# Pieces of work between the expert jobs of a mixture-of-experts kernel, and the row fetches, begun in later slots

## The chip, the cores and the metric

The kernel runs on one core of a Trainium2 chip. The metric is the device time of one execution in microseconds (us). An engine here is one of TensorE (matmuls; PE in the profile, PEld for its weight loads), VectorE (DVE), ScalarE (ACT), GpSimd (POOL), and SyncE (SP), which only issues DMAs. Each has its own queue of instructions, executed in the order in which they are written; they wait for each other by semaphores.

## The reference

Four layers on x of shape (4, 512, 128), float32, each with a residual addition and a layer norm before it:

```python
x = x + attn_a(_layernorm(x), W)          # 16 heads of 8, squared scores with gated decay
x = x + ffn(_layernorm(x), ...)           # mixture of experts
x = x + attn_b(_layernorm(x), ...)        # a gated recurrence along the sequence
x = x + ffn(_layernorm(x), ...)           # the same mixture of experts

def ffn(x, gate_w, expert_bias, w1, w2, w3):
    scores = softmax(xf @ gate_w.T)
    _, sel = top_k(scores + expert_bias, 2)        # 2 of 8 experts for each of 2048 tokens
    routed = xf[token_idx] * top_scores_sorted[:, None]
    # per expert: h = silu(xe @ w1) * (xe @ w3); out = h @ w2, hidden width 352
    return zeros_like(xf).at[token_idx].add(routed_out)

def attn_b(x, ...):
    # i, f, g = x @ Wi, x @ Wf, x @ Wg; a causal convolution of 4 taps on i and f
    # h = sigmoid(f) * h + silu(i) * (1 - sigmoid(f)) along the sequence
    return (h * rms(h) * g_norm_weight * silu(g)) @ Wo
```

## The kernel before

The first attention layer takes the first 265 us. From there on the kernel is a sequence of 92 expert **jobs**. A job is 128 rows (pairs of token and expert) that go through one expert. The mixture of experts is done by halves of the tokens (two batches of 512 each), and twice, so there are four halves, m = 0 to 3, of 23 jobs (`JOBS`): 0 and 1 are the first expert layer, 2 and 3 the second. Job J is slot s of half m, with J = 23 m + s. The first four jobs stand among the attention's work, the rest is written as a loop over J on each engine (`job_tensor`, `job_scalar`, `job_vector`, `jobs_pool`).

In the slot of job J, TensorE does the two up matmuls of J (L1263, L1266), then the transposes (L1229: the product of job J-1; L1233: the rows of job J+1), then the down matmul of job J-2 (L1279). ScalarE does the silu of J (L1333), evicts the transposes (`turned`, L1245) and the result of J-2 (`ysb`, L1340). VectorE multiplies (`hid`, L1394). POOL issues the indirect DMA that returns the rows of J to `token_out` (L1185), waiting for `ysb`, and then the gathers of rows of later jobs (L1177) from `scaled_rows` into one of 12 buffers. A gather for the first job of a half waits for that half's ids (`id_in`) and for its scaled rows. Before a half's first transpose TensorE also waits for the list of experts (`s_job`, made by stage `experts`).

**Pieces between jobs.** Each engine calls `between_tensor`, `between_scalar`, `between_vector` or `between_pool` at the end of a slot. In the halves m = 1 and 2 these prepare half m + 1, whose tokens are the two batches b = 2m-2 and 2m-1:

- `add x` adds the returned rows of half m-1 to the residual (L1204, L1205), once SyncE has loaded them back after the last return of half m-1 has landed (`back_sync`, L1198). Then `stats x` (L187 to L192), the root on POOL (`norm_root`, L198), `apply x` (L205), `turn x` (transposes L212, eviction L221).
- the recurrence layer: `project` (L1480, L1484), `sigmoids`, `recur`, `squares`, `finish` (L1534, L1538), `means`, `rms_pool` (L1549), `out` (L1557).
- `stats y`, root, `apply y`, `turn y`: the norm of the second expert layer.
- routing: `logits`, `softmax`, `exp`, `top`, `first`, `second`, `ranks`, `weigh`, `scale` (L1019, followed by the stores of the scaled rows), `slots`, `spread` (to L1095), `lanes` (two operations, L1101), `number` (16 matmuls, L999, in two parts of eight that each wait for one `lanes`), `ids` (six operations from L1106 to L1111), `experts` (L1114 to L1117).

`IN_LATER` says in which slot each piece stands; a pair is for the first and the second batch. Within one slot the order is that of the calls: in `between_vector` the first batch's `recur` stands before the second batch's `apply x`, and in `between_tensor` both `project` pieces stand before `turn x`. Half 0 has its own table, `IN_FIRST`. In half 3 only the additions of the first two batches remain (`ADDS_IN_LAST`); those of the last two stand after the last job. The slots in which POOL's pieces stand are written as numbers in `between_pool`; a POOL piece at slot s comes after the return of job s, which exists two slots later on the other engines. `fetch_behind(J)` gives the job after whose return the rows of J are gathered.

## Time and profile before

| | |
|---|---|
| median of 3 runs | 662.81 us (662.61 to 666.58) |
| profiled execution | 668.38 us, of which 666.6 us are its span |
| TensorE busy | 515.2 us (77%), mean granted clock 0.845 |
| VectorE, ScalarE, POOL busy | 341.1, 322.3, 305.8 us |
| DMA | 44.01 MB, mean 66 GB/s |

How to read it: times are those of one profiled execution, from its first instruction on. A row of the timeline says when an instruction (or some merged ones of one line) starts, how long it lasts, engine, line and operation, and in brackets how long the engine was idle before it and which instruction released it. "remote" means that the semaphore came without an instruction of the profile that explains it. A clock of 1.00 is 2.4 GHz, 0.50 is 1.2 GHz; ends of matmuls are modelled. The time between two silus is the length of a slot.

### The profile page before, as it was taken

The page shows a single profiled execution, that of the slowest core. Times are in us where ns is not written, and L with a number is a line of the kernel's source. Part 1 is how long each engine was busy: PE and PEld are TensorE (multiplying, and loading weights), DVE is VectorE, ACT ScalarE, POOL GpSimd, SP SyncE. Part 2 cuts the span into 40 slices and gives each one's busy share as a digit, 9 for nine tenths or more (in the row PEclk, how much of TensorE's full clock was granted, in tenths as well). Part 3 has the DMA queues.
Part 4 walks back from the last instruction along what each step waited for, and adds up shares of the span by engine and source line. Part 5 has one row for each costly group of instructions (what it writes and reads, how often), then busy time and mean ns, then how long its engine had stood idle before and what let it go on. Part 6 is the DMA issues. An engine that isn't in the chain of part 4 may idle for free. (4 is left out here: it accounts for less than half of the span.)

```text
span 666.6 us, 11448 instructions
## 1 busy us (share of the span) xinstructions
PE 515.2 (77%) x3845; PEld 357.1 (54%) x3861; DVE 341.1 (51%) x798; ACT 322.3 (48%) x620; POOL 305.8 (46%) x320
## 2 busy tenths in 40 slices
PE   2756888789787878888958797785979878587792
PEld 1433465466465545676746466663746666365561
DVE  4657967977969885425614424361532536122111
ACT  1553676576568758366423224462422346233441
POOL 3111464454444477264464326426422743646531
PEclk9865588678678769998997998997889899789987
DMA  5055244244279302013013001122200212322203
GB/s 133 11 126 84 64 82 75 64 82 75 65 153 242 85 22 62 26 44 100 25 44 90 25 13 36 29 80 71 65 21 8 40 29 80 94 61 59 44 22 110
DMA packets 36442, 44.01 MB, mean 66 GB/s; under 512 B 5900, under 2 KB 31012, under 8 KB 36388
## 3 DMA queue, kind: packets, MB, share of 16 engines
q1 hardware_dynamic: 30500, 31.22, 19.2%
q0 software_dynamic: 5888, 12.07, 7.7%
q8 instruction: 34, 0.56, 0.4%
q14 instruction: 20, 0.16, 0.1%
HBM read 26.43 MB, written 15.86 MB: 63 GB/s over the span
## 5 line engine op out<-in xcount | busy, mean ns | idle before, releaser
L1185 POOL DMA_INDIRECT token_out<-ysb,id_out x92 | 94.4, 1026 | 160.0 <-ACT ysb L1340 142.7
L1394 DVE TENSOR_TENSOR hid<-silu,ps 128x352 f32<-128x352 f32 x92 | 47.9, 521 | 199.9 <-PE ps L1266 91.2
L845 POOL TENSOR_TENSOR PP<-PP,E 128x512 f32<-128x512 f32 x64 | 83.8, 1309 | 102.5 <-ACT PP L799 102.3
L1263 PE MATMUL ps<-room,turned 128*128 x184 | 84.4, 543 | 51.1 <-ACT turned L1245 34.5
L762 DVE TENSOR_SCALAR A<-ps 128x1024 int32<-128x1024 int32 x80 | 96.8, 1217 | 24.1 <-PE ps L669 23.8
L799 ACT ACTIVATE PP<-A,feps 128x1024 f32<-128x1024 f32 x80 | 92.1, 1151 | 26.7 <-DVE A L762 26.6
L1177 POOL DMA_INDIRECT tiled<-scaled_rows,id_in x92 | 91.2, 991 | 25.2 <-issue 23.5
L1245 ACT ACTIVATE turned<-ps 128x512 f32<-128x512 f32 (+2 forms) x100 | 56.3, 563 | 87.0 <-PE ps L1233 48.0
L1279 PE MATMUL ps<-room,turned 128*128 x552 | 83.9, 292 | 3.6 <-issue 1.8
L1279 PEld LDWEIGHTS ps<-room,turned 128*128 128x128 f32 x552 | 75.4, 207 | 5.5 <-issue 5.5
L1266 PE MATMUL ps<-room,turned 128*128 x184 | 78.3, 511 | 0.0
L1333 ACT ACTIVATE silu<-ps 128x352 f32<-128x352 f32 x92 | 42.6, 463 | 73.8 <-PE ps L1263 64.0
L669 PE MATMUL ps<-QS,KS 96*128 96x128 bf16 (+2 forms) x448 | 62.0, 286 | 17.2 <-DVE A L762 11.4
L1263 PEld LDWEIGHTS ps<-room,turned 128*128 128x128 f32 x184 | 30.4, 207 | 64.7 <-issue 64.5
L669 PEld LDWEIGHTS ps<-QS,KS 96*128 96x128 bf16 x448 | 38.9, 115 | 32.7 <-issue 17.5
L1229 PEld LDWEIGHTS ps<-ident,hid 128*128 128x128 f32 x276 | 39.0, 153 | 28.7 <-issue 20.3
L1266 PEld LDWEIGHTS ps<-room,turned 128*128 128x128 f32 x184 | 38.4, 209 | 22.6 <-issue 5.6
L1229 PE MATMUL ps<-ident,hid 128*128 128x128 f32 x276 | 50.1, 295 | 0.0
L808 ACT ACTIVATE E<-ps 128x512 f32<-128x512 f32 x64 | 37.9, 593 | 12.2 <-remote 8.7
L690 PE MATMUL ps<-QS,KS 6*128 6x128 bf16 x256 | 30.3, 250 | 17.1 <-ACT E L808 16.8
L1340 ACT ACTIVATE ysb<-ps 128x128 f32<-128x128 f32 x92 | 25.5, 277 | 27.8 <-PE ps L1279 14.8
L706 PE MATMUL ps<-PP,vp 128*9 128x128 f32 x768 | 35.2, 354 | 0.0
(196 smaller groups left out, 669.9 us busy)
## 6 DMA issues: line engine op xcount, KB each, us to landing
QS<-parts SPq DMA_DIRECT2D x24, 192.0 KB
KS<-parts SPq DMA_DIRECT2D x24, 192.0 KB
parts<-room SPq DMA_DIRECT2D x32, 128.0 KB, 2.4
scaled_rows<-xT SPq DMA_DIRECT2D x8, 512.0 KB
yb<-token_out SPq DMA_DIRECT2D x8, 512.0 KB, 4.1
room<-in_L_ffn_w_dram SPq DMA_DIRECT2D x2, 1408.0 KB, 14.3
tiled<-scaled_rows,id_in POOLq DMA_INDIRECT x92
token_out<-ysb,id_out POOLq DMA_INDIRECT x92
```

What stands on the lines that cost most here:

```text
L669: return pe.matmul(bank[:, col:col + width], KS[0:96, slot, h, P * j:P * j + P], QS[0:96, slot, h, t0:t0 + width], start=True, stop=True)
L762: v.tensor_scalar(A[:, U % 3, :].bitcast(I32), ps[:, bank:bank + 2, :].rearrange("p k t -> p (k t)").bitcast(I32), 0x7fffffff, None, ALU.b ...
L799: a.activation(PP[:, G % 2, 2 * p:2 * p + 2, :].rearrange("p k t -> p (k t)"), A[:, U % 3, :], ACT.Square, bias=feps[:, G // NG:G // NG + ...
L845: g.tensor_tensor(w, w, E[:, hh % 4, :], MUL).then_inc(s_PD, 1)
L1177: g.indirect_dma_start(rows[:, J % ROWS, :], None, xs_d[m], bass.IndirectOffsetOnAxis(ap=id_in[:, m % 2, s:s + 1], axis=0)).then_inc(s_row ...
L1185: g.indirect_dma_start(yr_d[m], bass.IndirectOffsetOnAxis(ap=id_out[:, m % 2, s:s + 1], axis=0), ysb[:, J % OUTS, :], None).then_inc(s_ret ...
L1229: ins = pe.transpose(ps[:, BK_R, P * c:P * c + P], hid[:, J % 2, P * c:P * c + P], ident[:, :])
L1245: a.activation(turned[:, n % 2, c0:c1, :].rearrange("p c l -> p (c l)"), ps[:, BK_R, P * c0:P * c1], ACT.Copy).then_inc(s_t, 1)
L1263: pe.matmul(ps[:, BK_A, 0:HID], turned[:, n % 2, 3, :], w13[:, bass.ds(e, 1), 0, :].squeeze(1), start=True, stop=True).then_inc(s_AB, 1)
L1266: pe.matmul(ps[:, BK_B + J % 2, 0:HID], turned[:, n % 2, 3, :], w13[:, bass.ds(e, 1), 1, :].squeeze(1), start=True, stop=True).then_inc(s_ ...
L1279: ins = pe.matmul(ps[:, BK_Y, 0:P], turned[0:hw, n % 2, c, :], w2s[0:hw, bass.ds(e, 1), c, :].squeeze(1), start=(c == 0), stop=(c == len(H ...
L1394: v.tensor_tensor(hid[:, J % 2, 0:HID], silu[:, J % 2, :], ps[:, BK_B + J % 2, 0:HID], MUL).then_inc(s_hid, 1)
```

## The change

The slots of all pieces in the halves 1 and 2, of the additions in half 3 and of POOL's pieces are renumbered, and the rule for the gathers. Nothing else is changed; the order in which pieces are called within a slot is the same.

```diff
-        IN_LATER = {'add x': (2, 4), 'stats x': (3, 5), 'apply x': (4, 6), 'turn x': (5, 6), 'project': (6, 7),
-                    'sigmoids': (6, 7), 'recur': (6, 7), 'squares': (7, 8), 'finish': (7, 8), 'means': (7, 9), 'out': (8, 10),
-                    'stats y': (9, 11), 'apply y': (10, 12), 'turn y': (11, 12),
-                    'logits': 13, 'softmax': 14, 'exp': 14, 'top': 15, 'first': 15, 'second': 16, 'ranks': 16, 'weigh': 17,
-                    'scale': (17, 18), 'slots': 17, 'spread': 18, 'lanes': (19, 20), 'number': 20, 'ids': 21, 'experts': 21}
-        ADDS_IN_LAST = (4, 6)
+        IN_LATER = {'add x': (5, 6), 'stats x': (6, 7), 'apply x': (7, 8), 'turn x': (8, 9), 'project': (9, 10),
+                    'sigmoids': (9, 10), 'recur': (9, 10), 'squares': (10, 11), 'finish': (10, 11), 'means': (10, 12), 'out': (11, 13),
+                    'stats y': (12, 14), 'apply y': (13, 15), 'turn y': (14, 15),
+                    'logits': 16, 'softmax': 17, 'exp': 17, 'top': 18, 'first': 18, 'second': 19, 'ranks': 19, 'weigh': 20,
+                    'scale': (20, 21), 'slots': 20, 'spread': 21, 'lanes': (21, 22), 'number': 22, 'ids': 22, 'experts': 22}
+        ADDS_IN_LAST = (6, 7)
...
                 b = 2 * m - 2
-                if s == 1:
+                if s == 4:
                     norm_root(2, b)
-                if s == 3:
+                if s == 5:
                     norm_root(2, b + 1)
-                if s == 5:
+                if s == 8:
                     rms_pool(b)
-                if s == 7:
+                if s == 10:
                     rms_pool(b + 1)
                     norm_root(3, b)
-                if s == 9:
+                if s == 12:
                     norm_root(3, b + 1)
...
             m, s = divmod(J, JOBS)
-            return J - ROWS if m == 0 else max(JOBS * m - 4 + s // 2, J - 9)
+            return J - ROWS if m == 0 else max(JOBS * m - 3 + s // 2, J - 9)
```

So not every piece moves by three: `add x`, `stats x` and `apply x` of the second batch move by two, `lanes` and `number` by two, `ids` and `experts` by one. The first gathers of a half (m > 0) stand behind the return of slot 20 of the half before instead of slot 19, two gathers behind each return; the double gathers now go on to the returns of slots 0, 1 and 2 of the half itself.

## Rows read from the trace of the kernel before

**Rows 1.** Timeline, silus of slots 2 to 4 of half 1: start, length, instruction, [idle before]

```profile
354.30 0.47 ACT L1333 ACTIVATE silu<-ps 128x352 f32<-128x352 f32 x1 [1.71 <-PE ps L1263]
...
358.06 0.46 ACT L1333 ACTIVATE silu<-ps 128x352 f32<-128x352 f32 x1 [0.32 <-PE ps L1263]
...
360.72 0.47 ACT L1333 ACTIVATE silu<-ps 128x352 f32<-128x352 f32 x1 [0.68 <-issue]
```

**Rows 2.** Waits: engine, line waited for, us in total, times, longest us

```profile
DVE yb L1204 <- DMA yb<-token_out: 10.4, 1, 10.4
```

**Rows 3.** Chain that ended last, its end: start, us, what

```profile
654.71 2.25 DMA token_out<-ysb,id_out
...
657.15 3.96 DMA yb<-token_out
```

**Rows 4.** Timeline, the seam from half 1 to half 2

```profile
448.47 0.17 DVE L1106 COPY idh<-ps 128x23 f32<-128x23 f32 x1
...
449.54 0.18 DVE L1111 TENSOR_SCALAR id_in<-idf 128x23 uint32<-128x23 f32 x1
...
450.04 0.47 ACT L1333 ACTIVATE silu<-ps 128x352 f32<-128x352 f32 x1 [0.68 <-PE ps L1263]
...
454.46 0.27 PE L1233 MATMUL ps<-ident,tiled 128*128 128x128 f32 x1
...
456.80 0.46 ACT L1333 ACTIVATE silu<-ps 128x352 f32<-128x352 f32 x1 [1.69 <-PE ps L1266]
```

**Rows 5.** Timeline, behind the first two seams

```profile
349.65 0.96 POOL L1177 DMA_INDIRECT tiled<-scaled_rows,id_in  x1 [0.30 <-issue]
...
351.99 0.60 ACT L1245 ACTIVATE turned<-ps 128x512 f32<-128x512 f32 x1 [5.95 <-remote]
...
463.69 0.95 POOL L1177 DMA_INDIRECT tiled<-scaled_rows,id_in  x1 [0.30 <-issue]
...
466.79 0.60 ACT L1245 ACTIVATE turned<-ps 128x512 f32<-128x512 f32 x1 [6.61 <-remote]
```

**Rows 6.** Windows: stretch, length, busy of PE, PEld, DVE, ACT, POOL, clock, DMA

```profile
457.00:473.50 16.50, 8.72 (x25) 5.97 (x26) 2.85 (x5) 2.96 (x8) 6.35 (x7) 0.59 0.28 93
```

**Rows 7.** Timeline, slot 6 of half 1

```profile
378.58 1.11 DVE L205 TENSOR_SCALAR xh<-xt,mv,lnr 128x128 f32<-128x128 f32 x4
...
379.83 0.63 PE L212 MATMUL ps<-ident,xh 128*128 128x128 f32 x4 [3.79 <-DVE xh L205]
```

**Rows 8.** Timeline, slots 18 to 20 of half 1

```profile
438.12 0.44 ACT L1333 ACTIVATE silu<-ps 128x352 f32<-128x352 f32 x1
...
441.24 0.54 DVE L1095 TENSOR_TENSOR injobid<-injob,idlo 128x368 bf16<-128x368 bf16 x1
...
441.94 0.45 ACT L1333 ACTIVATE silu<-ps 128x352 f32<-128x352 f32 x1
...
444.99 1.22 DVE L1101 TENSOR_TENSOR rest<-iolane,lane 128x1024 bf16<-128x1024 f32 x1
...
446.27 0.37 PE L999 MATMUL ps<-injobid,rest 128*128 128x46 bf16 x8 [0.50 <-DVE rest L1101]
```

**Rows 9.** The page's groups: out<-in xcount, busy us, mean ns, idle before, releaser

```profile
L1177 POOL DMA_INDIRECT tiled<-scaled_rows,id_in x92 | 91.2, 991 | 25.2 <-issue 23.5
...
L1394 DVE TENSOR_TENSOR hid<-silu,ps 128x352 f32<-128x352 f32 x92 | 47.9, 521 | 199.9 <-PE ps L1266 91.2
```

**Rows 10.** Timeline, the seam from half 0 to half 1

```profile
337.55 0.28 ACT L1340 ACTIVATE ysb<-ps 128x128 f32<-128x128 f32 x1 [0.18 <-PE ps L1279]
...
339.41 0.99 POOL L1185 DMA_INDIRECT token_out<-ysb,id_out  x1 [0.30 <-issue]
...
340.33 0.28 PE L1233 MATMUL ps<-ident,tiled 128*128 128x128 f32 x1
```

**Rows 11.** Timeline, slot 4 of half 1

```profile
362.87 1.04 POOL L198 TENSOR_TENSOR lnr<-lnv,mhalf 128x4 f32<-128x4 f32 x1
...
364.02 1.13 DVE L205 TENSOR_SCALAR xh<-xt,mv,lnr 128x128 f32<-128x128 f32 x4 [2.13 <-POOL lnr L198]
```

## Prediction

> **What bounds the kernel now.** The change acts only on the 88 jobs from about 265 us on, so I read the waits first, then this stretch in the timeline. TensorE sets its pace. A plain slot lasts 2.66 us from one silu to the next [rows 1]: TensorE runs the two up matmuls, the transposes and the down matmuls with hardly a gap, while ScalarE and VectorE wait for it. A piece between jobs costs time where TensorE works on it or is made to wait for it.
>
> The wait that a later start of the pieces would most plainly remove is the row addition's: VectorE needs the returned rows of the half before, and `mix_vector` stands behind it. The profile names such a wait once, 10.4 us [rows 2], and the end of the chain of waits tells which it is: a last return of 2.25 us, a load of 3.96 us and then the additions after the last job [rows 3]. Those additions are not touched. In the halves themselves the rows were there when VectorE came for them. So this gain is nothing in this execution, and the sum has to come from the rest.
>
> Three things do cost time around the pieces. First, the seam: between the last silu of half 1 and the first of half 2 lie 6.76 us instead of 2.66 [rows 4]. Second, just behind each seam, ScalarE's eviction of the transposes in slot 1 waited 5.95 us and 6.61 us [rows 5], and behind the third a little less, three waits of some 18 us together; the releaser is "remote", so the profile doesn't say what TensorE was held by. In the stretch after the second seam TensorE was busy 8.72 of 16.5 us, at a mean granted clock of 0.59 [rows 6]. Third, in slot 6 TensorE waits 3.79 us for the normalised rows of the second batch [rows 7].
>
> **The change, part by part.** No arithmetic is added. I follow one half of the two middle ones, m = 1, with its own times.
>
> *Slot 6, now 9.* Old: `recur` of the first batch and `apply x` of the second are both in slot 6, in this order, so VectorE normalises at 378.58 only after the recurrence, and TensorE's `turn x` has waited 3.79 us when it starts at 379.83 [rows 7]. New: `apply x` of the second batch is in slot 8, `turn x` in 9 behind the projection of the first, whose long matmuls hide it. The wait goes: -3.8 us in each middle half. Its lower bound is nothing, if VectorE gets late by as much (below).
>
> *The front.* Slots 0 to 4 carry nothing; three slots more of 2.66 us stand here, 8.0 us. At the back slots 18 to 22 become 21 and 22. Old, silu of slot 18 to silu of slot 22 is 438.12 to 450.04, 11.9 us; new, slot 21 does what slot 18 did, so 22 follows at the distance of the old 19, 438.12 to 441.94, 3.8 us [rows 4, 8]. 3.8 + 8.0 - 11.9 = -0.1 us.
>
> *The seam behind a middle half.* The ids of the next half were ready before its first gather; now they are on the path. Counted from the old slot 18 as the new slot 21: `spread` ends at 441.8 [rows 8]; `lanes` twice, 1.22 each, and the last job's product, 0.52, to 444.8 [rows 8, 9]; the second eight matmuls of `number`, 0.4, with the handover to 445.3 [rows 8]; the six operations of `ids`, which last from 448.47 to 449.72, 1.25 us [rows 4], and a handover, to 446.7. Then POOL may gather: issue to landing I take from the return, 2.25 us [rows 3], so the first row lies there at about 449.1. Old, the first row's transpose at 454.46 led to the silu at 456.80, 2.34 us later [rows 4]; so the first silu comes at 451.5, 9.5 us after the one at 441.94. Old 6.76: +2.8 us. TensorE also stands still in slot 22 for some 3 us, waiting for `lanes`; that lies inside these 9.5. `experts`, four operations behind `ids`, ends before the row lands and costs nothing; were the row earlier, it would be next. Bounds: +1.3 (the issue order alone, next part) to +4.
>
> *The seam before half 1.* There the ids are ready (its table isn't changed), and only `fetch_behind` acts: the first gather stands behind the return of slot 20, not 19. That result is in SBUF at 337.83, the return can start at 338.1 instead of 339.41 since no gathers stand before it [rows 10]; an indirect DMA occupies POOL 0.99 us, and 0.3 pass before the next [rows 9]; so gather at 339.4, landing at 341.7, against a transpose at 340.33 [rows 10]: +1.4 us. Bounds 0 and +2.6 (two places in POOL's queue).
>
> *POOL's queue at the front.* After a half's first three returns there are now two gathers each, then one. A return with two gathers is 3.85 us of POOL, with one 2.57, against slots of 2.66. From the first return on, the fourth (of slot 4, before the root of the first batch) starts 3 x 3.85 + 2.57 = 14.1 us later, the root ends at 16.4. The slots would have it wanted at about 11.0. Old, the root at 362.87 kept VectorE's normalisation waiting 2.13 us [rows 11], and TensorE hardly noticed. New, VectorE is blocked some 4.2 us in slot 7, with `stats` of the other batch and the next job's product queued behind; the normalised rows come at 17.6 where TensorE asks for them at 15.6. I take +1.8 us for each middle half; bounds 0 (the long first slots let POOL catch up) and +3.5.
>
> *Adds in the last half.* Two additions of 1.4 us move from slots 4 and 6 to 6 and 7; VectorE works only 0.52 us on each job there [rows 9], so nothing. What it costs without this cover is under 1 us. The outputs' stores start later, still long before the end of the last half.
>
> Sum: 1.4 + 2 x (2.8 - 0.1 + 1.8 - 3.8) = +2.8 us. The profiled execution took 668.38 us, 666.6 of it the span, 5.6 more than the median of 662.81; I set the sum against the median as it stands: 665.6.
>
> **The waits in slot 1.** The sum leaves the three unnamed waits as they were, and they are the largest thing nearby, some 18 us in all. Two readings fit. They ended shortly after POOL's last gather of its seam burst (349.65 + 0.96 against 351.99, and 463.69 + 0.95 against 466.79: 1.4 and 2.15 us [rows 5]), and the second of them ended 10.0 us after its half's first silu (456.80 to 466.79 [rows 4, 5]). If they hang on the burst of gathers and returns, they shorten. In the first seam it is nine instructions of 1.29 us from 338.1 on, to 349.4 instead of 350.6, while TensorE is 1.4 later: -2.6. In the others it is eight instructions from 446.9 to 456.9, 5.4 us after the first silu instead of 464.64 - 456.80 = 7.8: -2.4 each. Together -7.4 us. If they hang on TensorE's own time after its idle stretch, nothing changes.
>
> **The rivals.**
> - *The unnamed waits follow POOL's burst*: 2.8 - 7.4 = -4.6, 658 us. For it: both end shortly behind it [rows 5]. Against: the distance varies, 1.4 and 2.15. If they vanish altogether, 2.8 - 18 gives 648.
> - *The additions do wait in ordinary runs*, which are 5.6 us faster than the profiled one: perhaps these 5.6 us are just what gives the load its time. Then the change saves at most some 1.5 us a half more, 661. Against it: no row shows such a wait.
> - *The clock, on the other side.* TensorE now idles longer before the half's first job. The granted clock behind the second seam was 0.59 in the mean [rows 6], nearer to 1.2 than to 2.4 GHz, and the slot behind the first, partly at the lower level, took 354.30 to 358.06, 3.76 us, where a plain one takes 2.66 [rows 1]: +1.1, and +2 for a slot wholly at it. Two more such slots behind each of three seams are +12, with the sum 678 us; over 1% it gets from two more in all at +2. Against it: the clock is already low there, so much of this is paid.
>   The Trainium skill, "TensorE: Matmul & The Clock Gate", on the HAM clock gate, has it that "the default state is throttled, and activity releases the throttle": by that rule the longer idle would lead to this rival, while five plain slots in front would help the clock back. The trace agrees as far as low clocks stand behind the seams.
> - *It does not do what it says*: the additions never waited, so the parts merely trade places. This is the case that I forecast, with small bills.
>
> **How the numbers follow.** Unnamed waits stay, sum as above: 0.47. They shorten with the burst: 0.18; vanish or nearly: 0.1. Additions wait in ordinary runs: 0.1. Clock: 0.15. The likeliest gives 665.6; with its own bounds, 1.4 or 0 to 2.6 for the first seam and from both ends of the others, it runs from 655 to 671. I put 665. The range 655 to 672 leaves out the vanishing waits below and most of the clock case above. One per cent is 6.6 us, about what a measurement of this kernel tells from no change. Faster by more: the vanishing waits and a part of the burst case, 0.18. Slower by more: the clock case and the tail of the sum, 0.18. Within: 0.64.
>
> **What would show it.** TensorE's wait for the normalised rows of the second batch in slot 9 is gone; VectorE's wait for POOL's root in slot 7 is about 4 us instead of 2.13; TensorE stands before `number` in slot 22; seams of about 9.5 us behind the middle halves, 1.4 more at the first; no wait of the row additions in either kernel. I would be wrong if the evictions in slot 1 waited much less or more than 5 to 6.6 us, or if the clock behind the seams fell further.

## The result and the profile after

| | before | after |
|---|---|---|
| median | 664.69 us (4 runs, 662.61 to 669.22) | 641.53 us (4 runs, 639.94 to 646.65) |
| profiled execution | 668.38 us, span 666.6 | 639.94 us, span 638.2 |
| TensorE busy, mean granted clock | 515.2 us, 0.845 | 494.3 us, 0.879 |

The ratio is 0.9656, with an interval of 0.9577 to 0.9735: faster, by 3.4%. Ratios and their intervals are taken without the slower executions of each kernel, so a ratio can differ from that of the medians beside it, and the profile of the kernel before is of a slower one, 5.6 us above the median on record ahead of the prediction.

I had said 665 us, in a range of 655 to 672. The range missed the time, and the forecast of no change was wrong on this chip. On two of the three other chips on which both kernels ran, their ratio was 1.0144 and 1.0037, on the third 0.9817; the experiments below show where the difference lies.

I measure both kernels by the starts of their 92 silus (L1333). "Seam" is from the silu of slot 22 to that of slot 0 of the next half, "slots 1 to 3" from the silu of slot 0 to that of slot 3, "slots 4 to 22" from that of slot 3 to that of slot 22. In us:

| | first silu | half 0 | seam | slots 1-3 | 4-22 | seam | slots 1-3 | 4-22 | seam | slots 1-3 | 4-22 | last silu |
|---|---|---|---|---|---|---|---|---|---|---|---|---|
| before | 265.8 | 70.1 | 6.0 | 16.1 | 92.0 | 6.8 | 16.7 | 92.6 | 7.1 | 16.3 | 60.1 | 649.6 |
| after | 259.1 | 69.7 | 8.1 | 8.7 | 89.2 | 9.8 | 8.0 | 88.3 | 9.8 | 9.3 | 60.9 | 621.0 |
| change | -6.7 | -0.4 | +2.0 | -7.4 | -2.7 | +3.0 | -8.7 | -4.4 | +2.7 | -7.0 | +0.9 | -28.6 |

From the first silu to the last it is -21.8 us: slots 1 to 3 give -23.0, the seams cost +7.8, the rest gives -6.6. The 6.7 us ahead of the first silu lie in the attention, which the change doesn't touch.

The first seam, against [rows 10]: timeline of the kernel after; start, length, instruction, idle before it and its releaser.

```profile
328.85 0.46 ACT L1333 ACTIVATE silu<-ps 128x352 f32<-128x352 f32 x1 [0.68 <-PE ps L1263]
...
332.26 0.99 POOL L1177 DMA_INDIRECT tiled<-scaled_rows,id_in  x1 [0.30 <-issue]
...
335.07 0.30 PE L1233 MATMUL ps<-ident,tiled 128*128 128x128 f32 x1 [1.69 <-DMA tiled<-scaled_rows,id_in]
...
336.93 0.46 ACT L1333 ACTIVATE silu<-ps 128x352 f32<-128x352 f32 x1 [1.24 <-PE ps L1263]
```

TensorE now waits 1.69 us for the first row, whose gather stands one return later. Just behind it, against [rows 1, 5] (same view):

```profile
340.26 0.47 ACT L1333 ACTIVATE silu<-ps 128x352 f32<-128x352 f32 x1 [1.71 <-issue]
...
342.98 0.46 ACT L1333 ACTIVATE silu<-ps 128x352 f32<-128x352 f32 x1 [1.03 <-issue]
...
344.00 0.60 ACT L1245 ACTIVATE turned<-ps 128x512 f32<-128x512 f32 x1 [0.56 <-PE ps L1233]
...
345.63 0.46 ACT L1333 ACTIVATE silu<-ps 128x352 f32<-128x352 f32 x1 [0.68 <-PE ps L1263]
...
356.75 0.60 ACT L1245 ACTIVATE turned<-ps 128x512 f32<-128x512 f32 x1 [3.70 <-remote]
```

The wait of 5.95 us in slot 1 is gone; the eviction comes 0.56 us after ScalarE's last work. But the kind of wait is not gone: a "remote" one of 3.70 us stands 13 us later. The unnamed waits in the list of waits, which before has as 32.8, 18.1 and 6.0 us for the same three lines (us in total, times, longest us):

```profile
ACT turned L1245 <- remote: 19.3, 7, 3.7
...
DVE hid L1394 <- remote: 14.9, 3, 5.9
...
ACT ysb L1340 <- remote: 10.6, 7, 2.5
```

The seam behind half 1, against [rows 4, 8]:

```profile
434.88 0.44 ACT L1333 ACTIVATE silu<-ps 128x352 f32<-128x352 f32 x1
...
437.48 0.37 PE L999 MATMUL ps<-injobid,rest 128*128 128x46 bf16 x8 [1.11 <-DVE rest L1101]
...
438.96 0.18 DVE L1111 TENSOR_SCALAR id_in<-idf 128x23 uint32<-128x23 f32 x1
...
439.42 0.99 POOL L1177 DMA_INDIRECT tiled<-scaled_rows,id_in  x1 [2.33 <-DVE id_in L1111]
...
442.20 0.45 PE L1233 MATMUL ps<-ident,tiled 128*128 128x128 f32 x1 [1.11 <-DMA tiled<-scaled_rows,id_in]
...
444.67 0.46 ACT L1333 ACTIVATE silu<-ps 128x352 f32<-128x352 f32 x1 [1.71 <-PE ps L1263]
```

This is the chain as worked out: `lanes`, `number`, `ids`, gather, first transpose. It takes 9.79 us from silu to silu, where I had 9.5. The stretch behind it, against [rows 6] (windows; busy us of PE, PEld, DVE, ACT, POOL, then the clock):

```profile
442.00:458.50 16.50, 14.09 (x60) 9.28 (x61) 2.60 (x5) 5.81 (x13) 10.62 (x11) 0.88 0.36 109
```

TensorE is busy 14.09 us of the 16.5 instead of 8.72, at a granted clock of 0.88 instead of 0.59.

The pieces of half 1, against [rows 7, 11], and the end, against [rows 2, 3] (timeline, then the chain that ended last, then the waits):

```profile
363.69 1.04 POOL L198 TENSOR_TENSOR lnr<-lnv,mhalf 128x4 f32<-128x4 f32 x1
364.84 1.14 DVE L205 TENSOR_SCALAR xh<-xt,mv,lnr 128x128 f32<-128x128 f32 x4 [0.88 <-POOL lnr L198]
...
377.20 0.60 PE L212 MATMUL ps<-ident,xh 128*128 128x128 f32 x4
```

```profile
626.15 2.24 DMA token_out<-ysb,id_out
628.58 4.11 DMA yb<-token_out
```

```profile
DVE yb L1204 <- DMA yb<-token_out: 10.5, 1, 10.5
```

TensorE takes up `turn x` of the second batch without a wait, where it had waited 3.79 us. The end is unchanged, and GpSimd's gathers cost what they did [rows 9]:

```profile
L1177 POOL DMA_INDIRECT tiled<-scaled_rows,id_in x92 | 91.0, 989 | 29.3 <-issue 23.3
```

### The profile page after: what moved, and what is told of

The parts are those of the page before. It is cut to its first block and busy times, and to the rows that moved or that the text cites. A ratio compares the mean times of both kernels' runs of the same rounds, so it can differ in the third digit from the quotient of the medians.

```text
span 638.2 us, 11448 instructions
## 1 busy us (share of the span) xinstructions
PE 494.3 (77%) x3845; PEld 343.4 (54%) x3861; DVE 340.3 (53%) x798; ACT 321.6 (50%) x620; POOL 303.0 (47%) x320
## 5 line engine op out<-in xcount | busy, mean ns | idle before, releaser
L1185 POOL DMA_INDIRECT token_out<-ysb,id_out x92 | 92.0, 1000 | 136.7 <-ACT ysb L1340 121.8
L1263 PE MATMUL ps<-room,turned 128*128 x184 | 83.3, 536 | 39.6 <-ACT turned L1245 20.5
L1279 PE MATMUL ps<-room,turned 128*128 x552 | 80.3, 283 | 5.1 <-ACT ysb L1340 4.8
L1333 ACT ACTIVATE silu<-ps 128x352 f32<-128x352 f32 x92 | 42.5, 462 | 67.3 <-PE ps L1263 54.0
L669 PE MATMUL ps<-QS,KS 96*128 96x128 bf16 (+2 forms) x448 | 61.1, 283 | 18.5 <-DVE A L762 11.8
L1279 PEld LDWEIGHTS ps<-room,turned 128*128 128x128 f32 x552 | 71.4, 197 | 7.0 <-issue 7.0
L1266 PE MATMUL ps<-room,turned 128*128 x184 | 74.6, 489 | 0.0
L1263 PEld LDWEIGHTS ps<-room,turned 128*128 128x128 f32 x184 | 29.4, 201 | 54.8 <-issue 54.6
L1229 PEld LDWEIGHTS ps<-ident,hid 128*128 128x128 f32 x276 | 36.5, 144 | 25.2 <-issue 15.6
L1266 PEld LDWEIGHTS ps<-room,turned 128*128 128x128 f32 x184 | 37.7, 205 | 22.1 <-issue 4.5
L1229 PE MATMUL ps<-ident,hid 128*128 128x128 f32 x276 | 46.6, 279 | 0.1
L808 ACT ACTIVATE E<-ps 128x512 f32<-128x512 f32 x64 | 37.9, 592 | 13.9 <-remote 9.8
L1340 ACT ACTIVATE ysb<-ps 128x128 f32<-128x128 f32 x92 | 25.5, 277 | 27.9 <-remote 10.6
L690 PEld LDWEIGHTS ps<-QS,KS 6*128 6x128 bf16 x256 | 16.9, 105 | 32.5 <-ACT E L808 26.2
## 6 DMA issues: line engine op xcount, KB each, us to landing
room<-in_L_ffn_w_dram SPq DMA_DIRECT2D x2, 1408.0 KB, 13.9
```

The lines of the kernel that those rows point to most:

```text
L669: return pe.matmul(bank[:, col:col + width], KS[0:96, slot, h, P * j:P * j + P], QS[0:96, slot, h, t0:t0 + width], start=True, stop=True)
L1185: g.indirect_dma_start(yr_d[m], bass.IndirectOffsetOnAxis(ap=id_out[:, m % 2, s:s + 1], axis=0), ysb[:, J % OUTS, :], None).then_inc(s_ret ...
L1229: ins = pe.transpose(ps[:, BK_R, P * c:P * c + P], hid[:, J % 2, P * c:P * c + P], ident[:, :])
L1263: pe.matmul(ps[:, BK_A, 0:HID], turned[:, n % 2, 3, :], w13[:, bass.ds(e, 1), 0, :].squeeze(1), start=True, stop=True).then_inc(s_AB, 1)
L1266: pe.matmul(ps[:, BK_B + J % 2, 0:HID], turned[:, n % 2, 3, :], w13[:, bass.ds(e, 1), 1, :].squeeze(1), start=True, stop=True).then_inc(s_ ...
L1279: ins = pe.matmul(ps[:, BK_Y, 0:P], turned[0:hw, n % 2, c, :], w2s[0:hw, bass.ds(e, 1), c, :].squeeze(1), start=(c == 0), stop=(c == len(H ...
```

## The experiments

The question was what makes the unnamed waits. An eviction that waits for "remote" starts up to several us after the end that the profile models for TensorE's matmuls; I call such a result **late**, by the time from that end to the start of the instruction that waits for it. In the kernel before, the late ones in slot 1 stand at the end of GpSimd's unbroken runs of 12 gathers and returns, 15 us each (first seam: 335.6 to 350.6, result at 351.99). The kernel after has a run of nine, 11 us, then a pause of 3 us, then another of nine; its late results stand in the second, from some 7 us into it on (`ysb` at 352.42, `turned` at 356.75). Theory A: the length of GpSimd's run makes TensorE's results late. Theory B: the slots of the pieces matter. Theory C: the clock.

These runs were made on five chips, 2 to 6 here in order; chip 1 is that of the result, which may be one of them. A ratio is always to before on the same chip. Only on chips 1, 4 and 5 is there a profile of before, so on chips 2, 3 and 6 the slots can be set only beside profiles from other chips.

**The two halves of the change** (chip 2; before there 657.66 us).

```diff
fetch_only:
-            return J - ROWS if m == 0 else max(JOBS * m - 4 + s // 2, J - 9)
+            return J - ROWS if m == 0 else max(JOBS * m - 3 + s // 2, J - 9)
pieces_only: the whole change, but with the old line for the fetches
```

> The kernel before with the new rule for the gathers alone (first gather of a half behind the return of slot 20 instead of 19). The pieces stay in their old slots. Theory A, the unnamed waits behind the seams come from POOL's run of back-to-back gathers and returns (12 instructions, 15 us in the kernel before, 8 or 9 in the kernel after): they go with this edit, 18 to 23 us less, about 643 us. Theory B, the pieces' slots did it: 1 to 4 us more than before from the later first rows, 664 to 668 us. Theory C, the granted clock behind the seams: TensorE's idle time is about as long as before, so no change, 660 to 666 us.

> The changed kernel with the old rule for the gathers: all pieces and the additions in their new slots, first gather behind the return of slot 19. Theory A: the run at the seam from half 0 to 1 is as long as before and its wait of about 6 us stays there; behind halves 1 and 2 the first gather waits for the ids, returns 20 to 22 queue behind it, so the run is long again and the waits stay, 660 to 668 us. Theory B: the gain is here, about 643 us. Theory C: 660 to 668 us.

`fetch_only`: 643.07 us, ratio 0.9766 (0.9684 to 0.9848). In its profile, of an execution of 652.10 us, slots 1 to 3 take 8.3, 9.1 and 9.4 us, the seams 8.6, 8.7 and 8.7. `pieces_only`: 651.45 us, ratio 1.0014 (0.9961 to 1.0067). Its slots 1 to 3 take 15.2, 12.1 and 11.9, its slots 4 to 22 86.8 and 87.8. The eviction in slot 1 (`fetch_only`, then `pieces_only`; timeline):

```profile
351.07 0.60 ACT L1245 ACTIVATE turned<-ps 128x512 f32<-128x512 f32 x1 [0.56 <-PE ps L1233]
```

```profile
350.03 0.60 ACT L1245 ACTIVATE turned<-ps 128x512 f32<-128x512 f32 x1 [5.93 <-remote]
```

So on this chip the gain is the one line of the fetches, and B falls: the pieces alone give none. Beside the first profile of before they gain within the halves (92.0 and 92.6 there) and give it back at the seams (9.8 and 10.6 against 6.8 and 7.1); that before took 92 us on this chip too is not shown (chip 5 has 88.0 and 87.6).

**More work for TensorE behind the seam** (chip 2). Six idle fp32 matmuls of 128 columns stand ahead of the up matmuls of slots 0 to 2.

```diff
+        def fill_tensor():
+            for k in range(6):
+                nc.tensor.matmul(ps[:, BK_I, 0:P], ident[:, :], ident[:, :], start=True, stop=True)
...
+            if m and s < 3:
+                fill_tensor()
```

> The kernel before with six idle matmuls of 128 columns ahead of the up matmuls in the first three slots of halves 1 to 3, into a free PSUM bank; their results are used by nobody. Theory C, the clock falls in TensorE's idle time at the seams and that makes the long waits: the clock stays at 1.00 behind the seams and the waits shrink, 645 to 658 us. Theory A: the waits stay; the fillers cost up to 0.7 us a slot, 663 to 672 us.

665.66 us, ratio 1.0124 (1.0014 to 1.0233). The seams grow to 11.8, 11.8 and 13.9 us, slots 1 to 3 still take 11.7, 12.7 and 11.4, and results are still late; here the first silu (L1339 in this kernel):

```profile
343.55 0.47 ACT L1339 ACTIVATE silu<-ps 128x352 f32<-128x352 f32 x1 [6.34 <-remote]
```

C falls: the granted clock was 1.00 for at least 25 us ahead of each of the three late first silus. The stretch ahead of the one at 343.55 (windows; busy us of PE, PEld, DVE, ACT, POOL, then the clock):

```profile
315.00:343.50 28.50, 24.39 (x158) 18.80 (x157) 9.56 (x28) 10.62 (x26) 15.19 (x16) 1.00 0.11 35
```

The same holds from 434.0 to 459.6 and from 499.0 to 573.2 us. So the waits begin at the full clock, and it falls to the lower level only at or behind their ends.

**One gather behind each return** (chip 2), with the rows of J behind the return of J - 4.

```diff
-            return J - ROWS if m == 0 else max(JOBS * m - 4 + s // 2, J - 9)
+            return J - ROWS if m == 0 else J - 4
```

> The kernel before with the gathers of halves 1 to 3 one behind each return, the rows of job J behind the return of job J-4, so that POOL has two indirect DMAs for each slot of 2.66 us and no pairs of gathers at the seams. Theory A: the unnamed waits at the seams go or shrink below 2 us each, 640 to 650 us. Theories B and C: no gain from it; rows come at the last moment, 663 to 675 us.

814.32 us, ratio 1.2419 (1.2318 to 1.252). This was my mistake. TensorE transposes the rows of J + 1 in the slot of J, and these are gathered only after the result of J - 3 has gone out, so every slot waits for a gather:

```profile
PE ps L1233 <- DMA tiled<-scaled_rows,id_in: 128.2, 53, 4.8
```

Slots 1 to 3 took 9.2, 7.3 and 7.4 us. One late result is left behind the seams: at the first, `turned` at 342.03 is late by 1.9 us, at the end of a run of eight in 10 us. TensorE was so idle in this kernel that little more follows.

**Shorter runs** (chip 3; before there 645.86 us, 637.65 to 662.87).

```diff
after_lead6, from after:
-            return J - ROWS if m == 0 else max(JOBS * m - 3 + s // 2, J - 9)
+            return J - ROWS if m == 0 else max(JOBS * m - 3 + s // 2, J - 6)
six_first, from before:
-            return J - ROWS if m == 0 else max(JOBS * m - 4 + s // 2, J - 9)
+            return J - ROWS if m == 0 else max(JOBS * m - 4 + s // 2 + (s >= 6), J - 9)
```

> The kernel after, with the fetch rule max(23m - 3 + s//2, J - 6): behind the returns of slots 20, 21, 22 two gathers each, then one behind each return, so six are under way ahead of a half instead of nine in slots -3 to 2. Theory A (GpSimd's long unbroken runs of indirect DMAs make the results of TensorE come late): the second run behind each seam of the kernel after (345.2 to 356.6 us, nine instructions, late result 4.8 us at its end) breaks up, since every slot now has one return and one gather, 2.3 us of a 2.66 us slot; the late evictions behind it (4.8, 4.6, 3.4 us) shrink to 2 us or less, and the kernel gains 2 to 8 us on the kernel after: ratio 0.955 to 0.965 to the kernel before where the kernel after stands at 0.966 to 0.97. Rival (the late results have nothing to do with the length of the runs): the late evictions stay in the same slots and the time is that of the kernel after within 2 us. Either way the later start of slots 4 to 8's gathers costs nothing if rows land six slots (16 us) ahead of use against a landing of 2.3 us.

> The kernel before, with one number of the fetch rule changed: from slot 6 on a row is gathered one return later, so the first gathers of a half start as early as before (behind the return of slot 19 of the half before), and six instead of eight stand before the half's own first return; the pieces are where they were. Theory A (length of GpSimd's unbroken run): the run of twelve instructions, 15 us, at each seam becomes shorter or gets a pause, the late evictions in slot 1 (6.2, 5.3, 3.8 us) shrink or vanish, slots 1 to 3 behind each seam take 8 to 11 us instead of 16, and the ratio to before comes to 0.97 to 0.985. Rival (it matters that the first gathers of a half stand behind a later return, so that TensorE itself starts the half later): nothing changes, slots 1 to 3 stay at 16 us and the ratio at 1.00.

`after_lead6`: 634.58 us, ratio 0.9874 (0.974 to 1.0009). Slots 1 to 3 have no late result; the first ones stand in slots 5 to 7 and are down to 1.2 to 1.8 us. Further on there are some of 2.0 and 2.1 us in the middle halves and up to 2.6 in half 3. Slots 4 to 22 take 82.4 and 86.0 us. The ratio is short of the 0.955 to 0.965 that I expected. `six_first`: 654.3 us, ratio 1.0228 (1.0148 to 1.0308): a miss. Its run is ten instructions, 12.5 us; slots 1 to 3 take 14.2, 12.9 and 13.7 us, with results late by 4.8, 3.4 and 2.9 us. The late results are smaller than with the run of twelve on chip 1, as A has it, yet the kernel was 2.3% slower than before on this chip. Before itself was some 19 us faster here than on chip 1 (medians of 645.86 and 664.69), and that was the first sign that it is not the same on every chip.

**More GpSimd work in a quiet stretch** (chip 3). Behind each return of slots 14 to 21 of half 3, where gathers have ended, stands one idle gather, or one idle power.

```diff
idle_gathers, from after:
+                if m == 3 and 14 <= s < 22:
+                    nc.gpsimd.indirect_dma_start(junk[:, s - 14, :], None, xs_d[m],
+                                                 bass.IndirectOffsetOnAxis(ap=id_in[:, m % 2, s:s + 1], axis=0)).then_inc(s_junk, 16)
idle_powers, from after:
+                if m == 3 and 14 <= s < 22:
+                    nc.gpsimd.tensor_tensor(junk[:, s - 14, 0:TB], lnv[:, 0:TB], mhalf[:, 0:TB], ALU.pow)
```

> The kernel after, with one idle extra gather (its rows go to a buffer that nobody reads) behind each return of slots 14 to 21 of half 3, a stretch where a slot takes a plain 2.66 us and no piece stands between jobs. It takes GpSimd from about 2.3 us to 3.6 us for each slot; eight of them are 10.3 us more work for GpSimd, of which it makes up 0.35 us a slot. Theory A (dense indirect DMAs make TensorE's results late): evictions or products late by 2 us and more appear in this stretch, where the kernel after has none over 1 us, and TensorE's slots there lengthen before any buffer runs out. Rival B (only the buffers that GpSimd fills late can hold TensorE): rows are gathered nine slots ahead, so a delay of 10 us never reaches the first engine; slots stay at 2.66 us, and the end moves by the late last returns alone, 0 to 3 us.

> The kernel after, with one idle power operation of GpSimd (128 x 4... elements, about 1.0 us, result not read) behind each return of slots 14 to 21 of half 3 in place of the extra gather: GpSimd is as busy without a pause, but with no more DMAs. Theory A in the form that counts GpSimd's DMAs (their descriptors or packets): no late evictions, slots of 2.66 us, time of the kernel after. Theory A in the form that counts GpSimd's unbroken busy time: late results by 2 us and more, as in the run with idle gathers. If neither shows them, the long runs of this kernel's seams need something else as well, such as the loads and stores at the seam.

647.56 and 647.32 us (two runs each; after was not run on this chip, so the times say nothing). The first added instruction is behind the return at 615.8 and 618.3 us. `ysb` there, first with gathers (its line is L1342), then with powers (L1341):

```profile
619.22 0.28 ACT L1342 ACTIVATE ysb<-ps 128x128 f32<-128x128 f32 x1 [2.27 <-remote]
...
628.36 0.28 ACT L1342 ACTIVATE ysb<-ps 128x128 f32<-128x128 f32 x1 [2.25 <-remote]
```

```profile
620.37 0.28 ACT L1341 ACTIVATE ysb<-ps 128x128 f32<-128x128 f32 x1 [0.88 <-PE ps L1280]
...
630.19 0.28 ACT L1341 ACTIVATE ysb<-ps 128x128 f32<-128x128 f32 x1
```

With gathers there is a late result in every third slot or so. With powers, each about as long as a gather (1.05 us), only the first `ysb` is late, by some 0.4 us: the interval into slot 18 is 3.10 us, and those behind it are plain. The kernel after without any addition has the same there on chips 5 and 6 (3.07 and 3.09 us), where its gathers have ended. That speaks for the DMAs and against the mere busy time. It is one profile of each, so a pointer, not a proof. In both, three slots of the stretch ahead, where each return has its gather, took 9.0 to 9.1 us instead of 3 x 2.66.

**All on one chip again** (chip 4; before there 633.0 us, 622.08 to 637.2).

```diff
after_triple, from after:
-            return J - ROWS if m == 0 else max(JOBS * m - 3 + s // 2, J - 9)
+            return J - ROWS if m == 0 else max(JOBS * m - 3 + s // 3, J - 9)
before_again, after_again: unchanged; lead6_again: after_lead6
```

> The kernel before once more, for a second profile of it and its own spread beside the three others on this chip. Theory A (a long unbroken run of indirect DMAs on GpSimd makes results of TensorE late): the run of twelve at each seam, 15 us, is in the program, so the three late evictions of the transposes in slot 1 are there again, 3.8 to 6.2 us late each, and slots 1 to 3 behind each seam take 15 to 17 us, whatever the time of the execution. Rival (they were a matter of that one execution, as its time of 668 us beside runs of 638 to 666 would allow): they are absent or half as long, and then the gain of the change was luck of the executions compared. Time 640 to 665 us, ratio 1.00.

> The kernel after once more, on the same chip. Theory A: slots 1 to 3 behind the seams take 8 to 9.5 us again (before 16), the seams 8.1, 9.8 and 9.8 us, late results come at the end of the second run of nine behind each seam, 3.4 to 4.8 us; the ratio to before is 0.965 to 0.98. Rival (luck of the executions compared): the ratio is within 0.99 to 1.01.

> The kernel after with the fetch rule max(23m - 3 + s//3, J - 9): behind the returns of slots 20, 21 and 22 stand three gathers each instead of two, and none or one behind the next ones; so the gathers start at the same place, but all nine are in the first run: 12 instructions and some 15 us without a pause, as in the kernel before, where the kernel after has 8 or 9 and 10 to 11 us. Theory A: the late evictions in slot 1 come back, 3 to 6 us each, slots 1 to 3 take 12 to 16 us instead of 8 to 9, and the ratio to before is 0.985 to 1.0. Rival (the place of the first gather behind the return of slot 20 is what mattered, not the length of the run): slots 1 to 3 stay at 8 to 9.5 us, the time is that of the kernel after within 3 us, and the second run behind the seam is shorter.

> The kernel after with one gather behind each return from slot 0 on (rule max(23m - 3 + s//2, J - 6)), once more, on the same chip as the kernel after. Theory A: it has fewer late results than the kernel after and is 3 to 9 us faster, ratio to before 0.955 to 0.97. Rival (the 7 us between the two profiles was spread of the executions): within 2 us of the kernel after.

| chip 4 | median | seam | slots 1-3 | 4-22 | seam | slots 1-3 | 4-22 | seam | slots 1-3 | 4-22 |
|---|---|---|---|---|---|---|---|---|---|---|
| before_again | 634.93 | 6.5 | 8.7 | 94.3 | 6.0 | 7.3 | 99.3 | 6.0 | 7.3 | 50.4 |
| after_again | 633.26 | 8.7 | 9.4 | 90.2 | 9.8 | 9.3 | 90.3 | 10.3 | 9.0 | 50.5 |
| after_triple | 615.92 | 8.0 | 8.7 | 82.8 | 9.8 | 8.0 | 81.2 | 9.9 | 9.3 | 50.5 |
| lead6_again | 616.78 | 8.7 | 9.3 | 82.9 | 9.8 | 8.0 | 81.2 | 9.9 | 8.0 | 50.5 |

Theory A fell here, and my expectations for all four missed. **No result of TensorE is late, in any of the four**: the lists of waits have no "remote" row for `turned`, `hid` or `ysb`. The runs of indirect DMAs are even longer than on chip 1, since no late result interrupts them: in `before_again` 16 in 20.6 us at the first seam, and 43 in 55.1 us in half 3. The last half's 19 plain intervals take 50.4 us, 2.65 each, instead of 60. And before and after are equal: after has 1.0144 (1.0017 to 1.0271) to before, and before run again has 1.0155 (1.0035 to 1.0274) to itself, which is how far two sets of one kernel lie apart here.

Three more things are plain once the late results are out of the way. First, the additions do wait in the kernel before (`before_again`; SPq is the load's issue):

```profile
344.29 0.80 SPq L1198 DMA_DIRECT2D yb<-token_out  x2
344.37 0.60 ACT L1245 ACTIVATE turned<-ps 128x512 f32<-128x512 f32 x1 [0.56 <-PE ps L1233]
...
348.70 0.69 DVE L1204 TENSOR_TENSOR yb<-yb 128x512 f32<-128x512 f32 x1 [4.18 <-DMA yb<-token_out]
```

```profile
459.08 0.69 DVE L1204 TENSOR_TENSOR yb<-yb 128x512 f32<-128x512 f32 x1 [6.91 <-DMA yb<-token_out]
```

```profile
DVE yb L1204 <- DMA yb<-token_out: 21.8, 4, 10.4
```

Second, the root is late in the kernel after. The first batch's normalisation in `after_again`, then in `after_triple`:

```profile
361.93 1.13 DVE L205 TENSOR_SCALAR xh<-xt,mv,lnr 128x128 f32<-128x128 f32 x4 [4.17 <-POOL lnr L198]
...
363.21 0.63 PE L212 MATMUL ps<-ident,xh 128*128 128x128 f32 x4 [2.79 <-DVE xh L205]
```

```profile
357.63 1.13 DVE L205 TENSOR_SCALAR xh<-xt,mv,lnr 128x128 f32<-128x128 f32 x4 [0.87 <-POOL lnr L198]
...
359.25 0.60 PE L212 MATMUL ps<-ident,xh 128*128 128x128 f32 x4
```

Third, much of what separates the kernels on this chip is the clock that TensorE was granted. Slot 9 to slot 10 of half 1 in `after_again` and in `after_triple`, then the three slots with the recurrence (slots 6 to 9) in `before_again` and the same work (slots 9 to 12) in `after_triple` (windows):

```profile
364.47:376.56 12.09, 12.09 (x37) 6.77 (x36) 3.56 (x9) 3.56 (x8) 5.99 (x6) 0.86 0.11 33
```

```profile
360.49:370.92 10.43, 10.43 (x37) 5.63 (x36) 3.25 (x9) 3.56 (x7) 5.73 (x6) 1.00 0.14 40
```

```profile
355.72:390.16 34.44, 29.87 (x115) 18.20 (x114) 11.73 (x30) 9.23 (x19) 10.87 (x12) 0.90 0.06 18
```

```profile
360.49:388.06 27.57, 26.79 (x115) 16.25 (x114) 10.02 (x21) 9.07 (x18) 10.54 (x11) 1.00 0.09 22
```

The matmuls are the same in number, and TensorE is busy 1.7 and 3.1 us longer with them where the clock was lower.

**A fifth chip** (before there 651.22 us, 639.39 to 660.49).

> The kernel before, a third profile. What the runs have left open is whether the late results of TensorE (no instruction explains them; 16 us for slots 1 to 3 behind each seam, 60 us for the 19 intervals of the last half's slots 3 to 22) go with the chip or with the kernel. They were in the first profiles and absent (8.7, 7.3, 7.3 us and 50.4 us) in the one beside which before and after took 633 us alike. Theory D (they are a matter of the chip, or of what goes on beside on it, and of the density of GpSimd's DMAs only where they are there at all): in one call all kernels have them or none has; with them before takes 650 to 669 us, without 622 to 640. Theory A (length of the run alone): not tenable any more, since a run of twelve showed none.

> The kernel after, a third profile. Theory D: if before_third shows late results, this one shows them too, with slots 1 to 3 at 8 to 9.5 us against 16, and the ratio is 0.96 to 0.98; if before_third shows none, this one shows none either, the ratio is 0.99 to 1.02, and the parts come out as in the clean pair: seams 8.7, 9.8, 10.3 us against 6.5, 6.0, 6.0; the middle halves from slot 3 to slot 22 at 90.3 us each against 94.3 and 99.3. Rival (execution by execution, whatever the chip): one has them and the other not.

> The kernel after with three gathers each behind the returns of slots 20, 21 and 22 (rule max(23m - 3 + s//3, J - 9)), once more. Root theory (the returns of slots 0 to 2 with two gathers each push the root of the first batch back in GpSimd's queue, and VectorE's normalisation and TensorE behind it with it; 5.71 + 12.10 us for slots 9 and 10 of the kernel after against 2.73 + 10.44 here): without late results 14 to 20 us faster than the kernel after, ratio 0.97 to 0.98. Theory A, where late results are there at all: its run of twelve brings back those in slot 1, slots 1 to 3 take 12 to 16 us, and it loses some 15 us of that lead. Rival: the lead is there with late results too.

| chip 5 | median | seam | slots 1-3 | 4-22 | seam | slots 1-3 | 4-22 | seam | slots 1-3 | 4-22 |
|---|---|---|---|---|---|---|---|---|---|---|
| before_third | 642.83 | 6.8 | 11.8 | 88.0 | 6.0 | 12.9 | 87.6 | 7.1 | 13.0 | 55.4 |
| after_third | 646.06 | 8.7 | 9.0 | 93.4 | 9.8 | 9.3 | 90.0 | 9.8 | 7.9 | 58.3 |
| triple_again | 643.78 | 8.7 | 12.7 | 82.8 | 10.0 | 12.0 | 84.9 | 9.8 | 10.5 | 60.7 |

Late results are there in all three, where chip 4 had them in none of four, so they don't go with the single execution (theory D). Whether they go with the chip or with the time at which it ran, and what else ran on it then, is not shown: each chip was used at one time only. The waits of `before_third`, whose row for `yb` has 11.4 us, one of 10.4 being the last one:

```profile
ACT turned L1245 <- remote: 15.9, 5, 4.5
...
DVE yb L1204 <- DMA yb<-token_out: 11.4, 3, 10.4
```

They are milder than on the first chip, and the ratio of after is 1.0037 (0.9968 to 1.0105), not the 0.96 to 0.98 that I had expected with late results. `triple_again` has them in slot 2, at the end of its run of 12:

```profile
350.44 0.60 ACT L1245 ACTIVATE turned<-ps 128x512 f32<-128x512 f32 x1 [3.46 <-remote]
```

and its slots 1 to 3 take 12.7, 12.0 and 10.5 us where chip 4 had 8.7, 8.0 and 9.3. So where a chip has late results, the length of the run decides whether they stand in slots 1 to 3; where it has none, the length is nothing. It doesn't decide what they cost in all: `after_third`, with runs of nine, has its late results in slots 5 to 8 instead, and slots 4 to 22 take 93.4 us there where `triple_again` has 82.8. The lead of `triple_again` over after is 2 us here and was 17 us there.

**Two versions on a sixth chip** (before there 652.86 us). `one_earlier` is after with every piece of the halves 1 and 2 one slot earlier, and the fetch rule of `after_triple`.

```diff
one_earlier, from after:
-        IN_LATER = {'add x': (5, 6), 'stats x': (6, 7), 'apply x': (7, 8), 'turn x': (8, 9), 'project': (9, 10),
+        IN_LATER = {'add x': (4, 5), 'stats x': (5, 6), 'apply x': (6, 7), 'turn x': (7, 8), 'project': (8, 9),
...
-                    'scale': (20, 21), 'slots': 20, 'spread': 21, 'lanes': (21, 22), 'number': 22, 'ids': 22, 'experts': 22}
+                    'scale': (19, 20), 'slots': 19, 'spread': 20, 'lanes': (20, 21), 'number': 21, 'ids': 21, 'experts': 21}
...
-            return J - ROWS if m == 0 else max(JOBS * m - 3 + s // 2, J - 9)
+            return J - ROWS if m == 0 else max(JOBS * m - 3 + s // 3, J - 9)
```

> The kernel after with every piece of the halves 1 and 2 one slot earlier (ids and experts of the next half in slot 21, additions in 4 and 5, GpSimd's pieces one return earlier) and the rule max(23m - 3 + s//3, J - 9), so that the gathers stand behind the returns of slots 20, 21, 22, three each. What the parts should give against the kernel after: the ids are ready before the return of slot 20 has gone, so the two seams behind middle halves go from 9.8 us to 7 to 8 us (-2 to -3 each); the additions in slot 4 find the rows loaded, since SyncE's load starts in slot 1 and lasts 4 us; the root stands behind no double gathers, so slots 9 and 10 of the kernel after lose 4.6 us a half where that chip has no late results. Sum: 12 to 18 us faster than the kernel after without late results; with late results its run of twelve brings some 3 to 4 us in slots 3 and 4 of each half, and the lead is 3 to 8 us.

> The kernel after with one gather behind each return from slot 0 on (max(23m - 3 + s//2, J - 6)). Theory (the long run of GpSimd's DMAs matters only on chips with late results, the late root everywhere): 14 to 19 us faster than the kernel after on a chip without late results, as in the earlier call (616.8 against 633.3), 5 to 10 us on one with them. Rival: equal to the kernel after there.

> The kernel after on a fifth chip, to set the two beside it and for the ratio to before. Theory D: the ratio goes by whether TensorE's results come late on this chip: with strong ones (slots 1 to 3 of before 16 us) 0.965 to 0.975, without 1.00 to 1.01, in between 0.985 to 1.0. This kernel's own slots 1 to 3 take 8 to 9.4 us in any case, and the seams 8.1 to 8.7, 9.8 and 9.8 to 10.3 us.

After: 641.21 us, ratio 0.9817 (0.9727 to 0.9908), with late results in its profile. `lead6_third`: 629.42 us, ratio 0.9651 (0.9556 to 0.9746). `one_earlier`: 647.52 us, ratio 0.9916 (0.9867 to 0.9965), 6 us slower than after: a miss. Its seams fall only to 9.4 and 8.9 us (9.8 and 10.4), while its run of 12 puts slots 1 to 3 at 12.7, 13.5 and 11.8 us (8.7, 8.0, 9.1). Against after, `lead6_third` gains in slots 4 to 22, 83.2 and 84.4 us instead of 89.2 and 88.3. It was the faster one by 16.5 us on chip 4 and by 11.8 here, and below before on all three chips on which it ran, though on two of them the interval just takes in 1: the version to keep.

## Why the prediction was wrong

**The failed step: the unnamed waits were left as they were.** It carried 0.47 of the chances, against 0.28 for the two cases in which they change. On the first chip they vanished from slots 1 to 3, -23.0 us in a net of -21.8. The rival "vanish" gave 648 us, with 0.1; the rival "follow the burst" had the right mechanism for this chip but priced it at -7.4 us in all, because it let a wait end a fixed time behind the burst. In fact, cut from twelve to eight or nine with a pause behind it, the run made no late result at all in this profile. What I read wrongly was [rows 5]. I had three waits of the same kind at the same place and took "the profile doesn't say" for "it stays". A stretch of 18 us whose cause isn't known, beside a change that moves the gathers in it, should have had a wide range on the fast side. Even the stated bounds of the sum, 655 to 671, don't follow from its parts: these give -5.2 to +17.4 us, or 657.6 to 680.2, and the measured 641.53 lies below either. What makes the waits, and so why they went, stays open; that the line of the fetches is what removes them, the two halves of the change show on chip 2.

**"The additions wait in ordinary runs", 0.1, was true where results come in time.** On chip 4 VectorE waits 4.18 and 6.91 us in the kernel before. The interval into slot 5 is 4.33 us in half 1, and those into slots 5 and 6 are 8.34 and 3.88 us in half 2, against 2.66: 8.6 us together. In the profile that I had, TensorE's late results gave the load its time [rows 2]. The row was rightly read for this execution; it did not hold for the program.

**The seams were right.** First seam: +1.4 predicted, +2.0 measured, +2.2 on chip 4. Behind the middle halves: +2.8 predicted; +3.0 and +2.7, on chip 4 +3.7 and +4.3, inside the bound of 4 or just over it. The ids end 4.3 us after the silu of slot 22 (434.88 to 439.14), where I had 4.8, and the first row is transposed after 7.3, where I had 7.2.

**The middle halves: both terms too small.** The sum had -2.1 us for each; measured were -2.7 and -4.4, on chip 4 -4.1 and -9.0, of which 8.6 in all are the additions' wait. *The root*: VectorE's wait of 4.2 us in slot 7 came as 4.17, but I let TensorE lose 1.8 us by it, and on chip 4 it lost more. Intervals 9 and 10 are 5.71 and 12.10 us against 2.73 and 10.44 in `after_triple`, 4.6 us in each middle half. 3.0 of it is standing still, 2.79 in the wait for the normalised rows; the other 1.7 is the clock, 0.86 against 1.00 in the windows above, just behind that wait. I had given such a wait no price for the clock. On the first chip that bill was absent: the late results gave GpSimd time, and VectorE waited 0.88 us. *Slot 6*: -3.8 predicted. The intervals into slots 7 to 9 of before are 15.57, 14.53 and 4.34 us on chip 4, those into 10 to 12 of `after_triple` 10.44, 12.80 and 4.33: -6.9 without the late root. The wait for `turn x` is gone as foreseen; the other 3.1 us are again the clock, 0.90 against 1.00, with TensorE busy 29.87 us instead of 26.79. In `after` against `before` on chip 1 it is 1.00 against 0.95 and 0.90.

**The clock, on the other side**, 0.15, did not come on the first chip. TensorE idles longer ahead of the half, as I said, but the stretch behind the second seam has 0.88 where before had 0.59 [rows 6]. So most of the low clock there went with the waits. By the Trainium skill, "TensorE: Matmul & The Clock Gate", on the HAM clock gate, activity releases the throttle: the trace agrees in that the clock rose where the wait went. On chip 4, where no waits hide it, the rival's mechanism is there at a small size: slots 1 to 3 behind the second and third seams have 0.76 and 0.79 in `after_again` and 1.00 in `before_again`, and they take 1.98 and 1.65 us more.

**The whole sum.** It said +2.8 us for a kernel whose unnamed waits do not change. On chip 4, where none is there, the stretch from the first to the last silu became 1.4 us longer (616.7 - 264.0 = 352.7 in `before_again`, 614.8 - 260.7 = 354.1 in `after_again`), and the medians are 634.9 and 633.3. So the arithmetic of the parts was about right in sum, partly because the misses cancel, and the 23 us came from the one thing that I had left unchanged.

## What to carry to other kernels

Give a stretch of unnamed waits that the change touches a case of its own with its full size, not the value "unchanged", and ask what stands at the end of it in the other queues. Where gathers and small operations share GpSimd's queue, put no more than one gather behind each return where an operation follows that another engine waits for: here six rows ahead instead of nine was worth 12 to 17 us. On chip 4 three gathers behind each of the three returns ahead of the half did as well, since they too stand clear of the root. Of their 16.5 us in the middle halves there 6.0 are standing still; in the other 10.5 TensorE had the lower clock in the same slots (10, 16, 17 and 21), and why it had in slots 16, 17 and 21 is not shown. Compare kernels on one chip and on more than one, since the same program took 622 to 669 us by chip and execution, and what a change gains by removing a disturbance is not there where there is none.

## What the runs showed of the hardware

- Results of TensorE can reach the other engines several us after their modelled end, on chips 1, 2, 3, 5 and 6, and on chip 4 not at all. Neither level of the clock explains it: in the kernel before, the four transposes between `hid` at 347.09 and `turned` at 351.99 us took 4.9 us, in a stretch granted as 2.4 GHz for its most part; the same step takes 0.4 us in a plain slot. At the second seam, `turned` at 466.79 is late by 5.3 us in a stretch granted as 1.2 GHz (0.50 from 460 to 473 us), and in `fill_seam` results are late at 1.00.
- Where it occurs, it mostly stands in or just behind runs of indirect DMAs. On the first chip evictions of `turned` were late by 3.8 to 6.2 us at runs of 12 in 15 us, by 3.4 to 4.8 at a second run of nine, and not at all at a first of 8 or 9; on chip 2 a first run of eight in 10 us gave 1.9. On chip 6 runs of six in 7.4 us, again and again, made `ysb` late by 0.7 to 2.0 us in every third slot, and three slots took 9.1 us instead of 8.0. On chip 4 runs of 16 in 20.6 us and of 43 in 55.1 us gave none. The loading of instructions is not the link: in the kernel before, its queues moved no packet from 340 to 353 us nor from 457.6 to 467 us, where results were late. What links the two, and why one chip was free of it, stays open.
- Where the granted clock was lower, the same matmuls took longer: 37 in 12.09 us at 0.86 and in 10.43 us at 1.00, 115 in 29.87 us at 0.90 and in 26.79 us at 1.00 (chip 4).
- An indirect DMA occupies GpSimd 0.99 us and 0.30 us pass before the next. The first gather behind the idle seam landed for TensorE 2.8 us after its issue (439.42 to 442.20).
